# Final pass of a four-layer kernel: output stores issued by SyncE, norm buffers for four groups, eight output tiles

## What is computed

```
x = _layernorm(x + _L1_ffn_ref(x, ...))

# _L1_ffn_ref, cut
Yf = Y.reshape(EC, d) * slots_w[:, None]
out = jnp.zeros((T, d), x.dtype).at[slots_token].add(Yf)
shared = silu(x @ shared_gate.T) * (x @ shared_up.T) @ shared_down.T
return (out + shared)

def _layernorm(x, axis=-1, eps=1e-05):
    m = jnp.mean(x, axis=axis, keepdims=True)
    v = jnp.var(x, axis=axis, keepdims=True)
    return (x - m) / jnp.sqrt(v + eps)
```

## Time and profile before

| | us |
|---|---|
| median of 3 runs | 2058.26 (2056.01 to 2059.78) |
| the profiled execution: its time | 2051.49 |
| the profiled execution: its span, first to last instruction | 2049.3 |
| busy in the span: TensorE / VectorE / ScalarE / GpSimd | 1906.0 / 1560.3 / 1052.6 / 835.8 |
| first load of the final pass issued | 2000.46 |
| first / last activation pair of the final pass starts | 2015.85 / 2043.63 |

### The profile page before, as it was taken

The page is one execution under the profiler, slowest core; times in us unless marked ns, Lnnn a source line. Parts: engine busy times, 40 slices in busy tenths (PEclk is TensorE's granted clock), DMA queues, the critical chain, the costliest instruction groups (busy, mean ns, idle before and its releaser), DMA issues. The chain is left out here.

```text
span 2049.3 us, 36824 instructions
## 1 busy us (share of the span) xinstructions
PE 1906.0 (93%) x12560; PEld 1711.6 (84%) x12560; DVE 1560.3 (76%) x4280; ACT 1052.6 (51%) x2677; POOL 835.8 (41%) x865
## 2 busy tenths in 40 slices
PE   7999999999999969999799999999999999977990
PEld 6888888888888858888589999999999999977980
DVE  8978778787887755565478888888888888865756
ACT  5434433333433333332377666666666666734763
POOL 2232323233232310000144466666666666654775
PEclk9999999999999989999799999999999999998995
DMA  3200000000000222743000010000000000125877
GB/s 124 83 1 32 21 11 32 1 32 1 32 21 1 75 77 84 252 153 126 20 12 17 20 39 25 20 21 19 19 18 19 19 18 14 38 72 152 207 145 248
DMA packets 101928, 118.82 MB, mean 58 GB/s; under 512 B 12551, under 2 KB 93643, under 8 KB 101104
## 3 DMA queue, kind: packets, MB, share of 16 engines
q1 hardware_dynamic: 84672, 104.16, 15.8%
q0 software_dynamic: 12288, 8.11, 2.6%
q10 hardware_dynamic: 4784, 4.21, 0.6%
HBM read 75.43 MB, written 57.10 MB: 65 GB/s over the span
## 5 line engine op out<-in xcount | busy, mean ns | idle before, releaser
L237 POOL TENSOR_TENSOR rwkv_gate<-rwkv_key,rwkv_gate 128x512 f32<-128x512 f32 x128 | 203.7, 1591 | 525.0 <-DVE rwkv_key L442 525.0
L1419 POOL TENSOR_TENSOR kept_raw<-kept_raw,mla_row_inv 128x512 f32<-128x512 f32 x192 | 199.2, 1038 | 302.2 <-DVE mla_row_inv L1771 301.0
L310 ACT ACTIVATE rwkv_gate<-rwkv_r 128x512 f32<-128x512 f32 x128 | 76.6, 598 | 400.6 <-DVE rwkv_o_low L363 398.1
L1576 ACT ACTIVATE kept_raw<-kept_raw,mla_least 128x256 f32<-128x256 f32 (+1 forms) x512 | 227.9, 446 | 90.8 <-DVE mla_least L1755 89.7
L1755 DVE CUSTOM_DVE_ANT_0 kept_raw<-mla_score,kept_mask 128x256 f32<-128x256 f32 (+1 forms) x512 | 156.8, 352 | 80.0 <-PE mla_score L2130 79.5
L427 DVE TENSOR_TENSOR rwkv_kv<-rwkv_v,rwkv_key 128x512 f32<-128x512 f32 x128 | 88.0, 688 | 125.7 <-PE rwkv_v L475 123.4
L434 DVE TENSOR_TENSOR_SCAN rwkv_state<-rwkv_decay_w,rwkv_kv 128x256 f32<-128x256 f32 x256 | 166.0, 690 | 4.1
L2130 PE MATMUL mla_score<-mla_k_high,mla_q_high 128*128 128x256 f32 (+1 forms) x512 | 155.3, 303 | 0.0
L492 PE MATMUL rwkv_out<-rwkv_w_high,rwkv_o_high 128*128 128x256 f32 x512 | 143.3, 280 | 5.8 <-DVE rwkv_o_low L363 5.8
L492 PE MATMUL rwkv_out<-rwkv_w_high,rwkv_o_low 128*128 128x256 f32 x512 | 144.6, 282 | 0.0
L492 PE MATMUL rwkv_out<-rwkv_w_low,rwkv_o_high 128*128 128x256 f32 x512 | 143.5, 280 | 0.0
(11 more groups left out here) (403 smaller groups left out, 6405.4 us busy)
## 6 DMA issues: line engine op xcount, KB each, us to landing
kept_raw<-in_experts SPq DMA_DIRECT2D x27, 384.0 KB, 4.9
kept_raw<-in_rkvo SPq DMA_DIRECT2D x16, 512.0 KB, 3.3
moe_y_in<-sums SPq DMA_DIRECT2D x32, 256.0 KB, 4.9
sums<-ffn_empty SPq DMA_DIRECT2D x12, 512.0 KB, 6.6
slots<-ffn_empty SPq DMA_DIRECT2D x16, 361.2 KB, 5.8
moe_e_rows<-slots SPq DMA_DIRECT2D x32, 180.6 KB, 3.6
kept_x_in<-x SPq DMA_DIRECT2D x18, 256.0 KB, 2.7
mla_x_res<-x SPq DMA_DIRECT2D x17, 256.0 KB, 2.9
```

The source lines that it names most:

```text
L237: nc.gpsimd.tensor_tensor(gate[:, c % 2, :], key[:, c % 2, :], gate[:, c % 2, :], ALU.mult).then_inc(gated_done, 1)
L1419: nc.gpsimd.tensor_tensor(unit, unit, row_inv[:, v % PR, 0:len(heads)].rearrange("p (h a) -> p h a", a=1) .to_broadcast([P, len(heads), ke ...
L1576: last = nc.scalar.activation(probs[:, v % PR, i * keys:(i + 1) * keys], masked[:, v % 2, i * keys:(i + 1) * keys], ACT.Exp, bias=least[:, ...
```

## The change

The store leaves `apply_norm`, and SyncE issues it, STORE_LAG = 10 units behind its loads: in SyncE's order store(0) stands behind load_sums(10), store(5) behind load_sums(15), and store(6) to store(15) behind all loads. Each store waits for `normed`. The small norm tiles have four buffers in place of two, with the wait of `variance` from g = 4 on and for group g - 4. `x_out` has eight buffers in place of four, and `stored` eight semaphores.

```diff
-OUTRING = 4
+STORE_LAG = SUMRING + 4
+OUTRING = 8
+NORMS = 4
...
-        stats = s.sb("stats", [P, 2, 2 * UT, 6])
-        moments = s.sb("moments", [P, 2, 2 * UT, 2])
+        stats = s.sb("stats", [P, NORMS, 2 * UT, 6])
+        moments = s.sb("moments", [P, NORMS, 2 * UT, 2])
...
-            for p in range(UNITS):
-                load_sums(p)
+            def store(p):
+                sp.wait_ge(normed, p + 1)
+                sp.dma_start(unit_rows(out, ORDER[p]), x_out[:, p % OUTRING, :, :]).then_inc(stored[p % OUTRING], 16)
+
+            for p in range(UNITS + STORE_LAG):
+                if p < UNITS:
+                    load_sums(p)
+                if p >= STORE_LAG:
+                    store(p - STORE_LAG)
...
                 last.then_inc(normed, 1)
-                act.wait_ge(normed, p + 1)
-                act.dma_start(unit_rows(out, ORDER[p]), x_out[:, p % OUTRING, :, :]).then_inc(stored[p % OUTRING], 16)
...
             def variance(g):
                 first, units = GROUPS[g]
-                if g >= 2:
-                    dve.wait_ge(normed, GROUPS[g - 1][0])
+                if g >= NORMS:
+                    dve.wait_ge(normed, GROUPS[g - NORMS + 1][0])
...
```

More of the change, by code:

```diff
@@ L2337, in moe_phase @@
         x_out = s.sb("x_out", [P, OUTRING, UT, D])
-        stats = s.sb("stats", [P, 2, 2 * UT, 6])
-        moments = s.sb("moments", [P, 2, 2 * UT, 2])
+        stats = s.sb("stats", [P, NORMS, 2 * UT, 6])
+        moments = s.sb("moments", [P, NORMS, 2 * UT, 2])
         minus_half = s.sb("minus_half", [P, 2 * UT])
-        var_eps = s.sb("var_eps", [P, 2, 2 * UT])
-        rstd = s.sb("rstd", [P, 2, 2 * UT])
-        shift = s.sb("shift", [P, 2, 2 * UT])
+        var_eps = s.sb("var_eps", [P, NORMS, 2 * UT])
+        rstd = s.sb("rstd", [P, NORMS, 2 * UT])
+        shift = s.sb("shift", [P, NORMS, 2 * UT])
         xt_ps = s.ps("xt")
@@ L2494, in rsqrt @@
                 pool.wait_ge(var_done, g + 1)
-                nc.gpsimd.tensor_tensor(rstd[:, g % 2, 0:w], var_eps[:, g % 2, 0:w], minus_half[:, 0:w], ALU.pow)\
+                nc.gpsimd.tensor_tensor(rstd[:, g % NORMS, 0:w], var_eps[:, g % NORMS, 0:w], minus_half[:, 0:w], ALU.pow)\
                     .then_inc(rstd_done, 1)
@@ L2612, in apply_norm @@
                     last = nc.scalar.activation(x_out[:, p % OUTRING, t, :], tiles(ORDER[p])[:, t, :], ACT.Identity,
-                                                scale=rstd[:, g % 2, at:at + 1], bias=shift[:, g % 2, at:at + 1])
+                                                scale=rstd[:, g % NORMS, at:at + 1], bias=shift[:, g % NORMS, at:at + 1])
                 last.then_inc(normed, 1)
-                act.wait_ge(normed, p + 1)
-                act.dma_start(unit_rows(out, ORDER[p]), x_out[:, p % OUTRING, :, :]).then_inc(stored[p % OUTRING], 16)
             for g, (first, units) in enumerate(GROUPS):
@@ L2722, in combine @@
                 for t in range(UT):
-                    nc.vector.bn_stats(stats[:, g % 2, (p - GROUPS[g][0]) * UT + t, :], tiles(n)[:, t, :])\
+                    nc.vector.bn_stats(stats[:, g % NORMS, (p - GROUPS[g][0]) * UT + t, :], tiles(n)[:, t, :])\
                         .then_inc(counted, 1)
@@ L2727, in variance @@
                 first, units = GROUPS[g]
-                if g >= 2:
-                    dve.wait_ge(normed, GROUPS[g - 1][0])
+                if g >= NORMS:
+                    dve.wait_ge(normed, GROUPS[g - NORMS + 1][0])
                 dve.wait_ge(counted, UT * (first + units))
                 for t in range(units * UT):
-                    last = nc.vector.bn_aggr(moments[:, g % 2, t, :], stats[:, g % 2, t, :])
+                    last = nc.vector.bn_aggr(moments[:, g % NORMS, t, :], stats[:, g % NORMS, t, :])
                 last.then_inc(stats_done, 1)
                 dve.wait_ge(stats_done, g + 1)
-                nc.vector.tensor_scalar(var_eps[:, g % 2, 0:units * UT], moments[:, g % 2, 0:units * UT, 1], LN_EPS, None,
+                nc.vector.tensor_scalar(var_eps[:, g % NORMS, 0:units * UT], moments[:, g % NORMS, 0:units * UT, 1], LN_EPS, None,
                                         ALU.add).then_inc(var_done, 1)
@@ L2740, in shift_mean @@
                 dve.wait_ge(rstd_done, g + 1)
-                nc.vector.scalar_tensor_tensor(shift[:, g % 2, 0:w], moments[:, g % 2, 0:w, 0], -1.0,
-                                               rstd[:, g % 2, 0:w], ALU.mult, ALU.mult).then_inc(shifted, 1)
+                nc.vector.scalar_tensor_tensor(shift[:, g % NORMS, 0:w], moments[:, g % NORMS, 0:w, 0], -1.0,
+                                               rstd[:, g % NORMS, 0:w], ALU.mult, ALU.mult).then_inc(shifted, 1)
             for g, (first, units) in enumerate(GROUPS):
```

## The result

The changed kernel has a median of 2052.79 us (18 runs, 2050.80 to 2058.08), beside 2057.20 for the kernel before on the same chips (18 runs, 2053.20 to 2060.54 and one slow run of 2165.97 that the ratio leaves out). The ratio is 0.9986, with a 95% interval of 0.9980 to 0.9992: 2.9 us less, 1.6 to 4.1. A change of 2.9 us is near the edge of what such a measurement can tell.

What follows compares the result with a forecast made beforehand. VectorE with GpSimd was taken to bound the pass until 2035, then a ScalarE-VectorE ring, with GpSimd's drain ending last. Stores gave 2.9 us, norm buffers 2.54, not added: 2.6 off 2058.26 makes 2055.7 us, range 2053.0 to 2058.8.

Steps and rivals of the forecast that it cites:

- The ring of ScalarE and VectorE: Final pass's tail: VectorE's aggregation waits for ScalarE's normalisations, 2.7 us in all, with ScalarE's stores inside the ring.
- Stores leave ScalarE: ScalarE, p = 10 to 15: a unit costs 1.00 to 1.19 us instead of 1.60; p = 15 starts 2.9 us earlier.
- the other branch: GpSimd's closing drain, starting with the last power: ends at 2045.3 if it keeps its 6.04 us, and sets the end.
- Four norm buffers: VectorE before groups 7 and 8: idle times of 1.38 and 1.37 us shrink by 1.27 each, 2.54 us together.
- Stores join SyncE: SyncE's queue: each 0.38 us issue moves there and finds room; load_sums(13) is held by 0.05 us at most.
- the slack of p = 13: GpSimd's add for p = 13, at 2029.65: its load lands at 2028.4 to 2029.4, 0.3 to 1.2 us of slack.
- a sign against me: Final pass: a wait for y_in after 2010 was listed among the signs that would show the forecast wrong.
- The barrier: Closing barrier: GpSimd's drain starts 2.54 us earlier and, keeping 6.04 us, sets the end 2.5 us earlier; 2.6 taken.
- the first rival: Closing barrier: GpSimd's drain has an end of its own, so no change, 2058.3 us; chance 0.10.
- Loads behind stores: load_sums(11) to (15): sharing a queue with stores lengthens landings; slower, 2060.3 us at landings of 14 us; chance 0.06.
- The locks: VectorE's var_eps against GpSimd's adds, groups 2 and 4: both locks vanish, 1.8 us more, 2053.9 us; chance 0.05.
- Hidden issue time: ScalarE's tail: store issue time was hidden, so units still come every 1.6 us, 2058.3 us; chance 0.03.

Runs made afterwards that it cites:

- drain_mid: The changed kernel with one more GpSimd drain after expert 15, 32 of 64 indirect DMAs behind it: closing drain 3.42 us, end 9.99 us after p = 10 against 11.49.
- norms_only: The changed kernel with the stores back on ScalarE, four norm buffers and eight output tiles kept: end 13.28 us after p = 10 against 11.49.

## Why the prediction was right

The forecast was 2.6 us less and 2055.7 us; the trace gives 2.51, the ratio 2.9 (1.6 to 4.1), the median 2052.79. The two medians are 4.4 us apart, more than the tail gives, and the new one is 2.9 below the forecast. The tail explains neither; the level of the same kernel moves by 2 to 3 us between sets of runs: 2058.26 for the kernel before in the first three runs, 2057.20 in 18, 2055.26 and 2055.89 beside the experiments.

*What bounds the kernel.* The ring of ScalarE and VectorE up to p = 15 is shown: both waits are gone with four buffers, and come back at half their size with two when the stores have left ScalarE.

*Stores leave ScalarE.* The bounds were 1.00 and 1.19 us a unit, and I took the middle. Measured: 1.00 to 1.01, the lower bound, set by the rows of the expert loop. ScalarE steps over a satisfied wait without a gap. p = 15 starts 5.00 us after p = 10 where the middle said 5.5. This term was mis-sized by 0.5 us, without effect, as the other branch set the end.

*Four norm buffers.* 2 x 1.27 = 2.54; measured 2.54 (6.53 to 3.99). The 0.10 us in it was borrowed from ScalarE's rows, and ScalarE in fact pays nothing for a satisfied wait; that VectorE stands about 0.11 us between its statistics and its aggregation (2042.58 + 0.75 = 2043.33 to 2043.44) made the number come out, which is luck. The last shift was forecast 4.72 us after p = 10 and came at 4.72.

*Stores join SyncE.* The issues fit between the loads, with less room than I gave them. Timeline of SyncE around load_sums(12), store(2), load_sums(13) and store(3):

```profile
2028.45 0.98 SPq L2455 DMA_DIRECT2D moe_y_in<-sums  x2
...
2029.47 0.47 SPq L2463 DMA_DIRECT2D out<-moe_x_out  x1
...
2029.99 1.06 SPq L2455 DMA_DIRECT2D moe_y_in<-sums  x2
...
2031.09 0.55 SPq L2463 DMA_DIRECT2D out<-moe_x_out  x1
```

load_sums(13) goes out 7.36 us after p = 0 starts, 7.20 in the kernel before: held by 0.16 us, where I said 0.05 at most: the two issues of load_sums(12) took 0.98 us here, and I had counted 0.87. It has no effect, by the slack of p = 13. The last store landed 2.1 us after its issue, as counted. GpSimd did wait for y_in after 2010, 0.8 us in two waits, which I had named as a sign against me; they are the adds for p = 2 and 3, ahead of the first store, and p = 0 starts 15.42 us after the first load as before (15.39).

*The barrier.* The drain kept its length, so its branch set the end, 2.54 us earlier less 0.03. This was the least certain step, and the forecast rested on it; the first rival (an end of its own, 0.10) is out, and drain_mid shows what the length is made of. For that rival I had set the 6.04 us against the 1.12 us of the first phase, and this comparison was misread: a power runs under that drain too, and takes nearly all of it (GpSimd, 742 to 745).

```profile
742.98 1.01 POOL L244 TENSOR_TENSOR rwkv_rstd<-rwkv_var_eps,rwkv_minus_half 128x4 f32<-128x4 f32 x1 [6.66 <-DVE rwkv_var_eps L388]
```

That drain ended 0.07 us behind the power, against 5.31 in this phase, so the comparison understated how odd the 6.04 us were.

*The rivals.* Loads behind stores (0.06): what I had priced, landings that grow in a shared queue, did not come. The ten issues of load_sums(11) to (15), with stores among them in the same queue (DMAs issued from 2025.2 to 2035), land after 5.1 us in the median, as in the kernel before, and the longest recorded took 5.7:

```profile
moe_y_in<-sums SPq DMA_DIRECT2D x10, 256.0 KB, 5.1
```

The loss at a lag of six is of another kind, SyncE's wait for `normed` ahead of a load. The locks (0.05): still there, 1.16 and 1.09 us. Hidden issue time (0.03): out, by norms_only against the change, 1.8 us apart.

## What to carry to other kernels

Look at who arrives last in the closing barrier, and how far behind the others are: an edit on one branch is worth only the distance to the next; here two edits that gave 0.7 and 1.2 us each by itself gave 2.5 together, and one line was worth 0.6 or 1.5 depending on the rest. If GpSimd issues indirect DMAs, look at the length of its drain at the end, and drain it once more where it idles. When stores move into the queue that issues loads, place each behind enough loads that its data is long ready: four units nearer turned a gain of 2.5 us into a loss of 1.9.

## What the runs showed of the hardware

GpSimd's closing DRAIN took 0.80, 3.42 and 6.04 us with 0, 32 and 64 indirect DMAs issued since its last drain, the same in every run to 0.01 us, though the last of them had landed some 39 us earlier; 0.69 us of each is the last power, which runs under it. Right after the 64 issues it ended 5.29 us behind the last. Neither adding nor the error check on indices changes it. In the attention phase of the same kernel 128 indirect DMAs left a drain of only 1.37 us, and why is open. An addition of 128x4 elements on VectorE took 0.17 us alone and up to 1.16 while GpSimd added in SBUF as a tensor_scalar, and 0.16 and 1.12 as a tensor_tensor.
